# A two-layer graph kernel: the last tiles of the softmax sums in another order, and the weighting of the exponentials shared between VectorE and GpSimd

## The chip, the cores and the metric

One NeuronCore of a Trainium2 chip runs the program. The metric is the device time of one execution in microseconds (us); lower is better. All times here are medians of repeated executions, or come from one profiled execution.

## The reference, cut to what matters

The input is 512 nodes of 1024 features and 8192 edges (src, dst). Layer 0 is a graph layer with attention over edges, layer 1 a normalised aggregation. What the change touches is the softmax over the edges that end in one node and what it feeds:

```python
feat  = concat([h[src], h[dst]], axis=1)               # 8192 x 2048
e_f   = relu(feat @ W_kind + b_kind)                   # kinds hh, oo, ho by edge range
logit = (e_f @ W_a + b_a)[:, 0]
m     = segment_max(logit, dst)
ex    = exp(logit - m[dst])
den   = segment_sum(ex, dst)
z_f   = segment_sum((ex / den[dst])[:, None] * h[src], dst)
h_new = relu(concat([h, z_f])[:128] @ W_hn + b_hn)     # head rows
o_new = relu(concat([h, z_f])[128:] @ W_on + b_on)     # the other rows
```

The kernel doesn't keep alpha per edge. Edges of one kind between the same pair of nodes have the same logit, so it builds for each kind a dense 512x512 matrix of logits and one of edge counts. The attention matrix is then, row by row, the sum over three kinds of count * exp(logit - row max), divided by its row sum.

## The kernel before, in words

**Stages.** The products h @ W_ho, W_oo and W_hh run as "chunks" of eight weight slices each (`chunk`, L807; matmuls at L818); tables of the products go to HBM. GpSimd gathers the two table rows of each edge (`gather_src` L396, `gather_dst` L403, `gather_add` L410). The 64 edge tiles of 128 edges are numbered 0 to 51 (kind ho), 52 to 61 (kind oo), 62 and 63 (kind hh); tiles 0 to 61 are gathered. For a gathered tile, VectorE's `edge(q)` (L1154) makes the logits: an odd tile takes an addition of two gathered rows (L1161) and a multiply with a row sum (L1166), an even one the multiply alone, since its addition was made in the gather. `split_logits(a, b)` (L1180) adds the bias and cuts the logits into three bf16-exact parts, five small instructions. `logit_onehots(q)` (L1193) writes two one-hot matrices per tile (source and destination), by two TENSOR_SCALAR instructions at L1197, into one of four slots. ScalarE's `logit_parts(q)` (L611) then writes three copies of the destination one-hot, each scaled by one part of the logit (three ACTIVATE at L616). TensorE's `add_logits` (L862) waits for `s_part` and multiplies the parts with the source one-hot into PSUM banks 0 to 3 (L768), after which the slot is free (`s_ohu`).

**Order around the change.** Stages 14 and 15 come behind the last chunk (13) that needs weights beside the sums. All engines follow hand-written tables, keyed by (stage, k): `SUM_AT` (L485) says which tiles TensorE sums, `ONEHOT_AT` builds the one-hots one step ahead of it, `EDGE_AT` (L501), `SPLIT_AT` (L509) and `KIND_AT` (L512) place VectorE's `edge`, `split_logits` and `copy_kind`. In one step VectorE does `copy_kind`, then `edge`, then `split_logits`, then `logit_onehots`. `SUM_AT` has tiles 44 to 51 at (14,0) to (14,3), the two hh tiles at (14,5), 52 to 55 at (14,6) and (14,7), 56 to 59 at (15,0) and (15,1), 60 at (15,2) and 61 at (15,3). After the last tile of a kind TensorE closes the banks (L791) and VectorE reads them (`copy_kind`, four instructions at L1219); only then TensorE opens the banks for the next kind (L787).

**TensorE's queue** runs `head_rows(0)` (L957, matmuls at L966, the first half of a product for the 128 head rows) between chunk 13 and stage 14, and `head_rows(1)` behind stage 15. **ScalarE's queue** has `keep_second_halves((1,))` (L595, L601), which waits for the end of chunk 13, ahead of all `logit_parts` of stages 14 and 15.

**Weighting.** After the last `copy_kind`, the row maximum is made (L1336 to L1338), ScalarE makes twelve exponentials, four row blocks k by three kinds t (L705), and VectorE, per row block: three TENSOR_TENSOR_REDUCE at L1344 (multiply with the counts, row sum into `den3`), the addition of kind 1 to kind 0 (L1348), the sum of the three row sums (L1349), a reciprocal (L1350), and the addition of kind 2 (L1351), which releases ScalarE's scaling by the reciprocal (L709). TensorE transposes the result (L983) and uses it in the products at L996. In GpSimd's queue there are, behind the last gather, eight loads of h into SBUF (L455, L456), two bias loads behind the last tile's sum (L372), and then loads that wait for later stages.

Of the kernel before, what the change touches and what calls it, by code (L numbers as in the profile page):

```python
# [7 lines left out]
ALU = mybir.AluOpType  # L8
ACT = mybir.ActivationFunctionType
AX = mybir.AxisListType  # L10
# [11 lines left out]
TINY = 1e-30  # L22
# [3 lines left out]
def gnn_kernel(nc, x, src, dst, W_hh, b_hh, W_oo, b_oo, W_ho, b_ho, W_a, b_a,  # L26
# [3 lines left out]
    NM = N // P  # L30
    KT = D // P
    NN = D // FB
    ET = E // P
# [5 lines left out]
    with ExitStack() as ctx:  # L39
        def sem(name):  # L40
            return ctx.enter_context(nc.semaphore(name))
# [29 lines left out]
        logit_d = sb("logit_d", [P, 3, NM, N], F32)  # L71
        count_d = sb("count_d", [P, 3, NM, N], U16)
# [3 lines left out]
        onehot = sb("onehot", [P, OS, 4, N], BF16, over="topsum")  # L76
# [3 lines left out]
        iota_f = sb("iota_f", [P, N], FP16)  # L80
# [17 lines left out]
        node_f = sb("node_f", [P, ET, 3], F32)  # L98
# [6 lines left out]
        lgs = sb("lgs", [P, 3, ET], F32)  # L105
# [7 lines left out]
        den3 = sb("den3", [P, NM, 3], F32)  # L113
        den = sb("den", [P, NM], F32)
        rden = sb("rden", [P, NM], F32)
# [58 lines left out]
        s_part = sem("onehot_parts_ready")  # L174
# [33 lines left out]
        s_kfree = sem("kind_banks_free")  # L208
        s_mx = sem("row_max_ready")
        s_exp = sem("exp_done")  # L210
        s_rden = sem("row_sums_ready")
        s_att = sem("attention_ready")
        s_top = sem("top_banks_free")
# [135 lines left out]
        def _(pool):  # L349
# [21 lines left out]
            def bias(place, b):  # L371
                pool.dma_start(bias2[:, place, :], b.rearrange("(a d) -> a d", a=1).partition_broadcast(P)).then_inc(s_bias, 16)  # L372
# [84 lines left out]
            pool.wait_ge(s_ohu, OS + 2 * ET)  # L457
            bias(0, b_hn)
            bias(1, b_on)
            pool.wait_ge(s_deg, 2)  # L460
            pool.wait_ge(s_adjs, 2)
            pool.wait_ge(s_hnc, NN)
# [35 lines left out]
        for (c, k), qs in SUM_AT.items():  # L498
# [3 lines left out]
        EDGE_AT |= {divmod(8 * KT + 2 * i, KT): (24 + i,) for i in range(16)}  # L502
        EDGE_AT |= {(11, 7): (40,)}
        EDGE_AT |= {divmod(12 * KT + (3 * i) // 2, KT): (41 + i,) for i in range(10)}
        EDGE_AT |= {(14, k): (51 + k,) for k in range(KT)}
        EDGE_AT |= {(15, k): (59 + k,) for k in range(3)}
        assert [q for at_ in sorted(EDGE_AT) for q in EDGE_AT[at_]] == list(range(TG))
        ADJ_AT = {(6, 1): (0, 0), (6, 3): (0, 1), (6, 5): (1, 0), (6, 7): (1, 1), (7, 2): (2, 0), (7, 5): (2, 1)}
        SPLIT_AT = {(5, 7): (0, 7), (6, 7): (7, 14), (7, 7): (14, 19), (8, 7): (19, 24), (9, 7): (24, 29), (10, 7): (29, 34),  # L509
                    (11, 7): (34, 41), (12, 3): (TG, ET), (12, 7): (41, 46), (13, 7): (46, 51), (14, 0): (51, 52), (14, 3): (52, 54),  # L510
                    (14, 5): (54, 56), (14, 6): (56, 58), (15, 0): (58, 60), (15, 1): (60, 61), (15, 2): (61, 62)}
        KIND_AT = {(14, 5): 0, (14, 6): 2}  # L512

        SLOT = {q: i % OS for q, i in ORDER.items()}

        FIRST_EARLY = 2 * 2 * KT
        EARLY_BUILT = (0, 1, 2, 9, 3, 4, 5, 6, 7, 8)
# [10 lines left out]
        def _(act):  # L528
# [66 lines left out]
            def keep_second_halves(ms):  # L595

                for m in ms:
                    if m == 1:
                        chunk_done(act, CH_EDGE + 1)
                        act.wait_ge(s_st[3], 16 * CH_HH)  # L600
                        nc.scalar.copy(stage[:, 3, :], ps[:, NM + m, :]).then_inc(s_copied, 1)  # L601
                    else:
                        nc.scalar.copy(topsum[:, m, FB:D], ps[:, NM + m, :]).then_inc(s_copied, 1)
# [7 lines left out]
            def logit_parts(q):  # L611

                act.wait_ge(s_oh, ET - 2 * len(EARLY_AT) + ORDER[q] + 1)
                s = SLOT[q]
                for i in (1, 2, 0):
                    ins = nc.scalar.mul(onehot[:, s, 1 + i, :], onehot[:, s, 1, :], lgs[:, i, q:q + 1])  # L616
                ins.then_inc(s_part, 1)
# [74 lines left out]
            for q in range(CH_EDGE + 2):  # L692
                edge_chunk(q)
            q = CH_EDGE + 2
            keep_second_halves((1,))
            for at_ in SUM_AT:
                if at_[0] >= q:
                    for t in SUM_AT[at_]:
                        logit_parts(t)
            act.wait_ge(s_ohu, OS + 2 * ET)  # L700
            keep_second_halves((2, 3))
            act.wait_ge(s_mx, 1)
# [46 lines left out]
        def _(pe):  # L749
# [111 lines left out]

            def add_logits(q, place, s):  # L862

                pe.wait_ge(s_part, ORDER[q] + 1)
                accumulate(reg[0], place, onehot[:, s], 3)

            def sums(c, k):

                for q in SUM_AT.get((c, k), ()):
                    if q in (TG, T_HO):  # L870
                        pe.wait_ge(s_kfree, NM if q == TG else 2 * NM)
                        open_masked(2 if q == TG else 1)
                    if q % TC == 0 or q in (TG, T_HO):
                        reg[0] = codes(q // TC, TC)
                    add_logits(q, q % TC, SLOT[q])
                    if q in LAST_OF_KIND:
                        close_banks(s_kind)
# [79 lines left out]
            def head_rows(n):  # L957

                if n == 0:
                    pe.wait_ge(s_ht, 1)  # L960
                    pe.wait_ge(s_degin, 1)
                else:
                    pe.wait_ge(s_copied, base + 4)
                for k in range(KT):
                    pe.wait_ge(s_raw[k], (CH_EDGE + 2 + n) * 16 + 16)
                    nc.tensor.matmul(ps[:, NM + n, :], hT[:, k, :], raw[:, k, :], start=(k == 0), stop=(k == KT - 1)).then_inc(s_hn, 1)  # L966
                pe.wait_ge(s_hn, n * KT + KT)
                pe.sem_inc(s_hnc, 1)

            head_rows(0)  # L970
            for c in (14, 15):
                for k in range(KT):
                    sums(c, k)
            head_rows(1)
            pe.wait_ge(s_dinv, 1)
# [77 lines left out]
        def _(dve):  # L1053
# [5 lines left out]
            def step(ins):  # L1059

                chain[0] += 1
                ins.then_inc(s_v, 1)
                dve.wait_ge(s_v, chain[0])
# [129 lines left out]
            def logit_onehots(q):  # L1193

                dve.wait_ge(s_ohu, ET + ORDER[q] + 1)
                for j, e in ((0, 0), (1, 2)):
                    ins = nc.vector.tensor_scalar(onehot[:, SLOT[q], j, :], iota_f[:, :], node_f[:, q, e:e + 1], None, ALU.is_equal)  # L1197
                ins.then_inc(s_oh, 1)

            def inverse_counts(t, h):  # L1200
# [137 lines left out]
            nc.vector.tensor_scalar(nmx[:, :], mx[:, :], -1.0, None, ALU.mult).then_inc(s_mx, 1)  # L1338
            q = CH_EDGE + 2

            for k in range(NM):
                for t in range(3):
                    dve.wait_ge(s_exp, 3 * k + t + 1)
                    ins = nc.vector.tensor_tensor_reduce(out=logit_d[:, t, k, :], in0=logit_d[:, t, k, :], in1=count_d[:, t, k, :],  # L1344
                                                         scale=1.0, scalar=TINY if t == 0 else 0.0, op0=ALU.mult, op1=ALU.add,
                                                         accum_out=den3[:, k, t:t + 1])
                step(ins)
                nc.vector.tensor_tensor(logit_d[:, 0, k, :], logit_d[:, 0, k, :], logit_d[:, 1, k, :], ALU.add)  # L1348
                step(nc.vector.tensor_reduce(den[:, k:k + 1], den3[:, k, :], AX.X, ALU.add))  # L1349
                nc.vector.reciprocal(rden[:, k:k + 1], den[:, k:k + 1])  # L1350
                nc.vector.tensor_tensor(logit_d[:, 0, k, :], logit_d[:, 0, k, :], logit_d[:, 2, k, :], ALU.add).then_inc(s_rden, 1)  # L1351
            dve.wait_ge(s_deg, 2)
            nc.vector.tensor_copy(wrow[:, :], ps[:, 6, 0:NM]).then_inc(s_dinv, 1)
            for k in range(NM):
# [142 lines left out]
```

## Time and profile before

| | us |
|---|---|
| median of 3 executions (604.33 to 607.87) | 604.45 |
| the profiled execution, own time | 605.15 |
| its span in the profile | 603.4 |

The span is what the profile shows from the first to the last instruction of the core; 1.75 us of the execution's own time lie outside it. The profile gives each instruction's engine, line and duration, and for idle time the instruction whose end released the engine. PE is TensorE, DVE is VectorE, ACT is ScalarE, POOL is GpSimd. PEclk is the granted clock of TensorE as a share of full speed: 1.00 is 2.4 GHz, 0.50 is 1.2 GHz.

### The profile page before, as it was taken

How to read it: one execution, taken by the hardware profiler on the slowest of the kernel's cores; microseconds unless marked ns; L12 is line 12 of the kernel's file. 1: busy time of each engine (PE TensorE's matmuls, PEld its weight loads, DVE VectorE, ACT ScalarE, POOL GpSimd, SP SyncE). 2: the span in 40 equal slices, each digit the busy share in tenths (PEclk: the TensorE clock that was granted, in tenths of full speed). 3: DMA queues.
4: the chain of work that ended last, by engine and by line, in shares of the span. 5: the costliest groups of instructions: out<-in, count | busy, mean ns of one | idle time of the engine just before them, and what ended most of it. 6: DMA issues, size and time to landing. Idle time of an engine off the chain costs nothing.

```text
span 603.4 us, 7247 instructions
## 1 busy us (share of the span) xinstructions
PE 533.4 (88%) x2132; PEld 365.2 (61%) x2137; DVE 425.3 (70%) x910; ACT 278.1 (46%) x439; POOL 184.4 (31%) x177
## 2 busy tenths in 40 slices
PE   1799989999997999979998699965686999999997
PEld 1688857777763677634443377621135887878885
DVE  6756337865479699598868877667957469888352
ACT  0723431211225998756427556474865355225200
POOL 3260030008366565354738464532120100000000
PEclk9799989999998899999998799987575999999999
DMA  8897275349999999999999999987092537403121
GB/s 307 316 386 285 113 263 208 132 151 264 390 335 349 364 290 313 355 317 352 368 342 319 365 317 317 305 242 174 7 375 107 210 115 265 144 2 99 41 87 52
DMA packets 55838, 146.95 MB, mean 244 GB/s; under 512 B 6770, under 2 KB 6898, under 8 KB 55410
## 3 DMA queue, kind: packets, MB, share of 16 engines
q0 software_dynamic: 22352, 81.28, 42.9%
q1 hardware_dynamic: 27936, 54.54, 25.5%
q10 hardware_dynamic: 5506, 10.56, 4.7%
q8 instruction: 27, 0.44, 0.3%
q14 instruction: 17, 0.14, 0.1%
HBM read 127.47 MB, written 18.87 MB: 243 GB/s over the span
## 4 chain that ended last, share of the span: by engine, by line
PE 69%; DVE 18%; ACT 7%; issue 4%; ACTq 1%; DMA 1%; DVEq 0%
PE ps L818 37%; PE ps L768 9%; PE ps L908 8%; PE ps L996 4%; PE ps L1049 4%; ACT onehot L616 4%; PE ps L1027 3%; DVE gath L1166 2%; DVE ring_l L1141 2%; DVE onehot L1197 1%; DVE logit_d L1344 1%; DVE gath L1161 1%; PE ps L791 1%; PE ps L966 1%; DVE logit_d L1219 1%
## 5 line engine op out<-in xcount | busy, mean ns | idle before, releaser
L818 PE MATMUL ps<-ring_h,actT_h 128*128 128x512 f32 x376 | 161.4, 429 | 4.5 <-DVE actT_l L1136 3.1
L616 ACT ACTIVATE onehot<-onehot,lgs 128x512 bf16<-128x512 bf16 x192 | 122.4, 710 | 63.5 <-DVE onehot L1197 63.0
L818 PE MATMUL ps<-ring_l,actT_h 128*128 128x512 f32 x376 | 149.3, 397 | 0.0
L818 PE MATMUL ps<-ring_h,actT_l 128*128 128x512 f32 x376 | 149.3, 397 | 0.0
L560 ACT CAST ring_h<-raw 128x512 fp32r<-128x512 f32 x128 | 76.0, 621 | 92.6 <-PE ps L818 64.1
L1141 DVE TENSOR_TENSOR ring_l<-raw,ring_h 128x512 fp32r<-128x512 f32 x128 | 85.3, 687 | 38.8 <-ACT ring_h L560 29.3
L768 PE MATMUL ps<-onehot 128*128 128x512 bf16 x267 | 81.3, 419 | 33.9 <-ACT onehot L616 28.0
L400 POOL DMA_INDIRECT gath<-tab_a,tabl_i x62 | 68.8, 1110 | 133.0 <-DVE gath L1166 76.0
L1166 DVE SCALAR_TENSOR_TENSOR gath<-gath,wa_b 128x1024 f32<-128x1024 f32 x62 | 75.9, 1225 | 19.4 <-DMA gath<-tab_b,tabl_i 18.3
L818 PEld LDWEIGHTS ps<-ring_h,actT_h 128*128 128x128 f32 x376 | 72.6, 193 | 26.8 <-DVE actT_l L1136 3.3
L818 PEld LDWEIGHTS ps<-ring_h,actT_l 128*128 128x128 f32 x376 | 72.3, 192 | 16.1
L818 PEld LDWEIGHTS ps<-ring_l,actT_h 128*128 128x128 f32 x376 | 72.6, 193 | 14.7
L414 POOL DMA_INDIRECT gath<-tab_b,tabl_i x31 | 54.8, 1768 | 71.6 <-DMA tab_b<-stage 44.9
L768 PEld LDWEIGHTS ps<-onehot 128*128 128x128 bf16 x269 | 22.5, 102 | 86.4 <-issue 75.9
L1197 DVE TENSOR_SCALAR onehot<-iota_f,node_f 128x512 bf16<-128x512 f16 x128 | 39.4, 356 | 9.8 <-PE ps L768 9.1
L1161 DVE TENSOR_TENSOR gath<-gath 128x1024 f32<-128x1024 f32 x31 | 37.8, 1220 | 4.2 <-DMA gath<-tab_b,tabl_i 4.0
L407 POOL DMA_INDIRECT gath<-tab_b,tabl_i x31 | 33.4, 1078 | 9.4 <-issue 8.8
L908 PE MATMUL ps<-raw,featT_dst 128*128 128x512 f32 x64 | 30.0, 607 | 0.0
L908 PE MATMUL ps<-raw,featT_src 128*128 128x512 f32 x64 | 29.1, 592 | 0.0
L1089 DVE TENSOR_SCALAR onehot<-iota_f,node_f 128x512 bf16<-128x512 f16 x44 | 16.1, 365 | 15.9 <-PE ps L768 13.9
L1131 DVE TENSOR_TENSOR actT_l<-ps,actT_h 128x512 fp32r<-128x512 f32 x16 | 11.0, 690 | 14.3 <-ACT actT_h L550 14.3
L578 ACT COPY stage<-ps 128x512 f32<-128x512 f32 x16 | 9.4, 585 | 24.4 <-PE ps L818 19.0
(199 smaller groups left out, 632.9 us busy)
## 6 DMA issues: line engine op xcount, KB each, us to landing
raw<-in_L_gnn_W_ho_dram SPq DMA_DIRECT2D x32, 256.0 KB
raw<-in_L_gnn_W_oo_dram SPq DMA_DIRECT2D x32, 256.0 KB
raw<-in_L_gnn_W_hh_dram SPq DMA_DIRECT2D x32, 256.0 KB
raw<-in_L_gnn_W_on_dram SPq DMA_DIRECT2D x32, 256.0 KB
raw<-in_L_gnn_W_hn_dram SPq DMA_DIRECT2D x32, 256.0 KB
tab_a<-stage ACTq DMA_DIRECT2D x16, 256.0 KB
tab_b<-stage ACTq DMA_DIRECT2D x16, 256.0 KB
raw<-in_L_gnn_W_dram SPq DMA_DIRECT2D x16, 256.0 KB
```

The lines of the kernel that those rows point to most:

```text
L400: pool.indirect_dma_start(out=gath[:, c % GB, :], out_offset=None, in_=tab_a[0:kinds * N, :], in_offset=bass.IndirectOffsetOnAxis(ap=tabl_ ...
L407: pool.indirect_dma_start(out=gath[:, c % GB, :], out_offset=None, in_=tab_b[0:kinds * N, :], in_offset=bass.IndirectOffsetOnAxis(ap=tabl_ ...
L414: pool.indirect_dma_start(out=gath[:, c % GB, :], out_offset=None, in_=tab_b[0:kinds * N, :], in_offset=bass.IndirectOffsetOnAxis(ap=tabl_ ...
L560: nc.scalar.copy(ring_h[:, k, :], raw[:, k % RAW, :]).then_inc(s_high, 1)
L616: ins = nc.scalar.mul(onehot[:, s, 1 + i, :], onehot[:, s, 1, :], lgs[:, i, q:q + 1])
L768: mm = nc.tensor.matmul(ps[:, bass.ds((lo + j) & 3, 1), :].rearrange("p a n -> p (a n)"), rows[:, 1 + i, j * P:(j + 1) * P], rows[:, 0, :] ...
L818: mm = nc.tensor.matmul(ps[:, first + m, :], w, v, start=(k == 0 and i == 0), stop=(k == KT - 1 and i == 2))
L908: mm = nc.tensor.matmul(ps[:, b, :], featT[half][:, k, t * P:(t + 1) * P], raw[:, k, :], start=(half == 0 and k == 0), stop=(half == 1 and ...
L1141: nc.vector.tensor_tensor(ring_l[:, k, :], raw[:, k % RAW, :], f32(ring_h[:, k, :]), ALU.subtract).then_inc(s_low, 1)
L1161: nc.vector.tensor_tensor(gath[:, c % GB, :], gath[:, c % GB, :], gath[:, d % GB, :], ALU.add).then_inc(s_sum, 1)
L1166: nc.vector.scalar_tensor_tensor(out=gath[:, c % GB, :], in0=gath[:, c % GB, :], scalar=0.0, in1=wa_b[:, :], op0=ALU.max, op1=ALU.mult, ac ...
L1197: ins = nc.vector.tensor_scalar(onehot[:, SLOT[q], j, :], iota_f[:, :], node_f[:, q, e:e + 1], None, ALU.is_equal)
```

## The change

1. Edges: tile 52 joins tile 51 in step (14,0), and all later tiles are made one step earlier; tiles 60 and 61 are split together in (15,1).
2. For tiles 57, 59 and 61 (`SCALED`) VectorE itself writes the three scaled one-hots from `iota_f`, by three TENSOR_SCALAR with compare and multiply, in place of the one plain destination one-hot; ScalarE leaves these tiles out. TensorE waits for `s_oh` for them, and for the renumbered `s_part` (`PART_NO`) for the others.
3. `keep_second_halves((1,))` moves on ScalarE from ahead of stage 14 to behind the parts of step (14,3).
4. `head_rows(0)` moves on TensorE from ahead of stage 14 to ahead of the sums of step (14,2).
5. Weighting: VectorE's three instructions per row block become plain TENSOR_TENSOR multiplies. GpSimd adds kind 1 to kind 0. `row_sum(k)` on VectorE adds kind 2 with the row sum taken in the same instruction, adds TINY, and takes the reciprocal, which now releases ScalarE. It stands behind the first multiply of the next row block.

```diff
@@ gpsimd, behind the two bias loads
+            for k in range(NM):
+                pool.wait_ge(s_weight, 3 * k + 2)
+                nc.gpsimd.tensor_tensor(logit_d[:, 0, k, :], logit_d[:, 0, k, :], logit_d[:, 1, k, :], ALU.add).then_inc(s_pair, 1)
@@ tables
-        EDGE_AT |= {(14, k): (51 + k,) for k in range(KT)}
-        EDGE_AT |= {(15, k): (59 + k,) for k in range(3)}
+        EDGE_AT |= {(14, 0): (51, 52)}
+        EDGE_AT |= {(14, k): (52 + k,) for k in range(1, KT)}
+        EDGE_AT |= {(15, 0): (60,), (15, 1): (61,)}
-                    (14, 5): (54, 56), (14, 6): (56, 58), (15, 0): (58, 60), (15, 1): (60, 61), (15, 2): (61, 62)}
+                    (14, 5): (54, 56), (14, 6): (56, 58), (15, 0): (58, 60), (15, 1): (60, 62)}
+        SCALED = (57, 59, 61)
+        PART_NO = {q: i + 1 for i, q in enumerate(q for q in SUMS if q not in SCALED)}
@@ scalar
-            keep_second_halves((1,))
             for at_ in SUM_AT:
                 if at_[0] >= q:
                     for t in SUM_AT[at_]:
-                        logit_parts(t)
+                        if t not in SCALED:
+                            logit_parts(t)
+                    if at_ == (14, 3):
+                        keep_second_halves((1,))
@@ tensor, add_logits
-                pe.wait_ge(s_part, ORDER[q] + 1)
+                if q in SCALED:
+                    pe.wait_ge(s_oh, ET - 2 * len(EARLY_AT) + ORDER[q] + 1)
+                else:
+                    pe.wait_ge(s_part, PART_NO[q])
@@ tensor
-            head_rows(0)
             for c in (14, 15):
                 for k in range(KT):
+                    if (c, k) == (14, 2):
+                        head_rows(0)
                     sums(c, k)
@@ vector, logit_onehots
+                if q in SCALED:
+                    for i in range(3):
+                        ins = nc.vector.tensor_scalar(onehot[:, s, 1 + i, :], iota_f[:, :], node_f[:, q, 2:3], lgs[:, i, q:q + 1],
+                                                      ALU.is_equal, ALU.mult)
+                else:
+                    ins = nc.vector.tensor_scalar(onehot[:, s, 1, :], iota_f[:, :], node_f[:, q, 2:3], None, ALU.is_equal)
@@ vector, weighting
+            def row_sum(k):
+
+                dve.wait_ge(s_pair, k + 1)
+                dve.wait_ge(s_weight, 3 * k + 3)
+                step(nc.vector.scalar_tensor_tensor(out=logit_d[:, 0, k, :], in0=logit_d[:, 0, k, :], scalar=1.0, in1=logit_d[:, 2, k, :],
+                                                    op0=ALU.mult, op1=ALU.add, accum_out=den[:, k:k + 1]))
+                step(nc.vector.tensor_scalar(den[:, k:k + 1], den[:, k:k + 1], TINY, None, ALU.add))
+                nc.vector.reciprocal(rden[:, k:k + 1], den[:, k:k + 1]).then_inc(s_rden, 1)
+
             for k in range(NM):
                 for t in range(3):
                     dve.wait_ge(s_exp, 3 * k + t + 1)
-                    ins = nc.vector.tensor_tensor_reduce(...)
-                step(ins)
-                nc.vector.tensor_tensor(logit_d[:, 0, k, :], logit_d[:, 0, k, :], logit_d[:, 1, k, :], ALU.add)
-                step(nc.vector.tensor_reduce(den[:, k:k + 1], den3[:, k, :], AX.X, ALU.add))
-                nc.vector.reciprocal(rden[:, k:k + 1], den[:, k:k + 1])
-                nc.vector.tensor_tensor(logit_d[:, 0, k, :], logit_d[:, 0, k, :], logit_d[:, 2, k, :], ALU.add).then_inc(s_rden, 1)
+                    nc.vector.tensor_tensor(logit_d[:, t, k, :], logit_d[:, t, k, :], count_d[:, t, k, :], ALU.mult).then_inc(s_weight, 1)
+                    if k and t == 0:
+                        row_sum(k - 1)
+            row_sum(NM - 1)
```

## Rows read from the trace of the kernel before

**Rows 1.** Windows: us, then busy us (instructions) per engine, PEclk, DMA share, GB/s

```profile
core 0: us, PE busy (x) PEld busy (x) DVE busy (x) ACT busy (x) POOL busy (x), PEclk, DMA share, GB/s
...
388.00:396.00 8.00, 7.11 (x19) 2.82 (x18) 0.00 (x0) 7.93 (x13) 2.29 (x2) 1.00 0.94 272
...
404.00:412.00 8.00, 4.03 (x10) 1.17 (x10) 6.62 (x16) 4.50 (x8) 6.59 (x5) 0.51 0.84 207
```

**Rows 2.** Waits, 387 to 463 us: us in total, times, longest

```profile
ACT onehot L616 <- DVE onehot L1197: 13.0, 5, 5.0
...
PE ps L768 <- ACT onehot L616: 10.0, 6, 4.2
```

**Rows 3.** Timeline of TensorE, 378 to 475 us: start, duration, engine, line, operation

```profile
387.84 7.03 PE L966 MATMUL ps<-raw,hT 128*128 128x512 f32 x16
395.75 3.04 PE L768 MATMUL ps<-onehot 128*128 128x512 bf16 x12 [0.89 <-PE ps L966]
...
412.90 2.22 PE L768 MATMUL ps<-onehot 128*128 128x512 bf16 x6
...
439.59 1.46 PE L768 MATMUL ps<-onehot 128*128 128x512 bf16 x3 [1.75 <-ACT onehot L616]
...
442.55 8.33 PE L966 MATMUL ps<-raw,hT 128*128 128x512 f32 x16
```

**Rows 4.** Timeline of ScalarE, 372 to 475 us

```profile
388.04 0.58 ACT L601 COPY stage<-ps 128x512 f32<-128x512 f32 x1 [8.03 <-PE ps L818]
388.52 7.45 ACT L616 ACTIVATE onehot<-onehot,lgs 128x512 bf16<-128x512 bf16 x12
...
422.71 12.97 ACT L616 ACTIVATE onehot<-onehot,lgs 128x512 bf16<-128x512 bf16 x21 [5.00 <-DVE onehot L1197]
```

**Rows 5.** Timeline of VectorE, 372 to 443 us

```profile
380.40 1.38 DVE L1197 TENSOR_SCALAR onehot<-iota_f,node_f 128x512 bf16<-128x512 f16 x4
...
408.63 0.69 DVE L1219 CUSTOM_DVE_ANT_0 logit_d<-ps,logit_d 128x512 f32<-128x512 f32 x1 [1.35 <-PE ps L791]
...
411.07 1.22 DVE L1166 SCALAR_TENSOR_TENSOR gath<-gath,wa_b 128x1024 f32<-128x1024 f32 x1
...
416.02 0.69 DVE L1219 CUSTOM_DVE_ANT_0 logit_d<-ps,logit_d 128x512 f32<-128x512 f32 x1 [1.60 <-PE ps L791]
...
418.47 1.22 DVE L1161 TENSOR_TENSOR gath<-gath 128x1024 f32<-128x1024 f32 x1
...
421.00 0.23 DVE L1187 TENSOR_SCALAR lgr<-lg,ba 128x2 f32<-128x2 f32 x1
...
422.06 1.14 DVE L1197 TENSOR_SCALAR onehot<-iota_f,node_f 128x512 bf16<-128x512 f16 x4
...
442.79 0.69 DVE L1219 CUSTOM_DVE_ANT_0 logit_d<-ps,logit_d 128x512 f32<-128x512 f32 x1 [5.88 <-PE ps L791]
```

**Rows 6.** Groups by line and shape on VectorE: busy us, mean ns, idle before

```profile
L1119 DVE TENSOR_SCALAR hrow<-rows,mv,rstd 128x1024 f32<-128x1024 f32 x4 | 3.0, 808 | 0.0
```

**Rows 7.** Timeline of VectorE, the weighting, 446 to 461 us

```profile
446.71 0.69 DVE L1344 CUSTOM_DVE_ANT_0 logit_d<-logit_d,count_d 128x512 f32<-128x512 f32 x1 [0.79 <-ACT logit_d L705]
...
448.67 0.69 DVE L1348 TENSOR_TENSOR logit_d<-logit_d 128x512 f32<-128x512 f32 x1
449.28 0.15 DVE L1349 TENSOR_REDUCE den<-den 128x1 f32<-128x3 f32 x1
449.46 0.16 DVE L1350 RECIPROCAL rden<-den 128x1 f32<-128x1 f32 x1
...
450.13 0.68 DVE L1344 CUSTOM_DVE_ANT_0 logit_d<-logit_d,count_d 128x512 f32<-128x512 f32 x1
...
459.78 0.67 DVE L1351 TENSOR_TENSOR logit_d<-logit_d 128x512 f32<-128x512 f32 x1
```

**Rows 8.** Timeline of GpSimd, single instructions at both ends of the run

```profile
2.54 0.29 POOL L358 CAST ident_b<-ident 128x128 bf16<-128x128 f32 x1
...
3.29 0.09 POOL L364 MEMSET ones<- 128x1 f32 x1
...
29.22 6.39 POOL L380 DMA_INDIRECT hh_rows<-h_rows,hh_i  x1 [0.30 <-issue]
...
379.88 1.56 POOL L414 DMA_INDIRECT gath<-tab_b,tabl_i  x1 [0.31 <-issue]
```

More of the change, by code:

```diff
@@ L210, in gnn_kernel @@
         s_exp = sem("exp_done")
+        s_weight = sem("kinds_weighted")
+        s_pair = sem("two_kinds_summed")
         s_rden = sem("row_sums_ready")
@@ L1195, in logit_onehots @@
                 dve.wait_ge(s_ohu, ET + ORDER[q] + 1)
-                for j, e in ((0, 0), (1, 2)):
-                    ins = nc.vector.tensor_scalar(onehot[:, SLOT[q], j, :], iota_f[:, :], node_f[:, q, e:e + 1], None, ALU.is_equal)
+                s = SLOT[q]
+                ins = nc.vector.tensor_scalar(onehot[:, s, 0, :], iota_f[:, :], node_f[:, q, 0:1], None, ALU.is_equal)
+                if q in SCALED:
[4 more added lines that the diff above has]
+                    ins = nc.vector.tensor_scalar(onehot[:, s, 1, :], iota_f[:, :], node_f[:, q, 2:3], None, ALU.is_equal)
                 ins.then_inc(s_oh, 1)
@@ L1343, in _ @@
                     dve.wait_ge(s_exp, 3 * k + t + 1)
-                    ins = nc.vector.tensor_tensor_reduce(out=logit_d[:, t, k, :], in0=logit_d[:, t, k, :], in1=count_d[:, t, k, :],
-                                                         scale=1.0, scalar=TINY if t == 0 else 0.0, op0=ALU.mult, op1=ALU.add,
-                                                         accum_out=den3[:, k, t:t + 1])
-                step(ins)
-                nc.vector.tensor_tensor(logit_d[:, 0, k, :], logit_d[:, 0, k, :], logit_d[:, 1, k, :], ALU.add)
-                step(nc.vector.tensor_reduce(den[:, k:k + 1], den3[:, k, :], AX.X, ALU.add))
-                nc.vector.reciprocal(rden[:, k:k + 1], den[:, k:k + 1])
-                nc.vector.tensor_tensor(logit_d[:, 0, k, :], logit_d[:, 0, k, :], logit_d[:, 2, k, :], ALU.add).then_inc(s_rden, 1)
+                    nc.vector.tensor_tensor(logit_d[:, t, k, :], logit_d[:, t, k, :], count_d[:, t, k, :], ALU.mult).then_inc(s_weight, 1)
+                    if k and t == 0:
+                        row_sum(k - 1)
+            row_sum(NM - 1)
             dve.wait_ge(s_deg, 2)
```

## The prediction

> **What bounds the kernel now.** I read the windows first, to see where TensorE is not full, then the waits of that stretch, then the timelines of its engines. From 404 us TensorE does 4.03 us of work in 8 and its granted clock falls to 0.51, the lower of its two levels (1.2 GHz) [rows 1]: it waits. The waits say for whom: TensorE 10.0 us for ScalarE's scaled one-hots, and ScalarE 13.0 us for VectorE's plain ones [rows 2]. So between 388 us and the last read of the banks at 442.79 us the time is set by a chain that passes VectorE, ScalarE and TensorE in turn, through four slots. Two places stand out. ScalarE sits idle for 8.03 us until 388.04, on a copy that waits for chunk 13, while the one-hots of tile 44 had been there since about 381 us; the parts of tiles 44 to 47 are made only beside head_rows(0), and those of 48 to 51 only after it [rows 3, 4, 5]. And from 422.71 us ScalarE makes 21 scaled copies in one run of 12.97 us, seven tiles at 1.85 us each [rows 4]: there it is the bound. Behind 442.79 us the chain is VectorE's weighting, 446.71 to 460.45 [rows 7]. It sets the end: TensorE only transposes what that releases. Head_rows(1), 442.55 to 450.9 [rows 3], lies beside the weighting and is covered.
>
> **Stages 14 and 15, first part (edits 3 and 4).** I lay the new order along the clock of the trace. Chunk 13 still ends at about 388.0. ScalarE no longer waits for it: 44 from 381.2, 45 to 385.0. Edge 52 now stands ahead of the one-hots of 46 and 47 and costs 1.15 us (the row of 1.22 less its overlap [rows 5]); they are ready at 387.1 and 387.6, the parts at 389.0 and 390.9. TensorE does 44 and 45 at once and reaches 47 at about 391.6, for it starts 0.69 us behind the end of its parts (ScalarE's last part ended at 438.90, the tile's sum began at 439.59 [rows 3]). A tile takes 0.76 us (twelve matmuls in 3.04 [rows 3]): 392.4. Head_rows(0) takes 7.03 us: 399.5. In its shadow VectorE makes the one-hots of 48 and 49 behind edge 53 (390.1) and those of 50 and 51 once 47's slot is free, and ScalarE their parts, 390.9 to 398.4, four times 1.87. So behind head_rows(0) nothing is waited for: a gap of 0.9, four tiles 3.04, closing the banks 0.9 (sums end at 412.90 + 2.22, the read starts at 416.02 [rows 3, 5]), and copy_kind(0) starts at **404.3 in place of 408.63: 4.3 us earlier**. The moved copy (0.58 us) sits at about 398.5 on ScalarE, idle until the hh tiles are due, and only head_rows(1) needs it. What head_rows(0) releases is the load of eight weight slices for head_rows(1), 4.6 us later, used 40 us later. GpSimd's gathers run ahead: the last ones go out as slots come free, edge by edge, so they move with the edges, some 15 us ahead of use. Nothing else waits in either queue.
>
> The hh tiles: from the end of copy_kind(0) to copy_kind(2) is 4.95 us (411.07 to 416.02), opening, two tiles, closing [rows 5]. New: 406.75 + 4.95 = 411.7. VectorE in between has edge 57, now an odd one, 2.53 (418.47 to 421.00), a split 1.06, four one-hots 1.06 [rows 5]: ready at 411.4, just hidden. A later copy_kind(2) of some tenths is possible; it starts at 411.7, still 4.3 us early, and ends at 414.15.
>
> **Second part (edits 1 and 2).** From here VectorE alone sets the pace. Two even edges at 1.15, two odd at 2.53, three splits at 1.07 instead of four, and the one-hots: 54 and 55 four instructions, 56 and 57 six, 58 and 59 six, 60 two, 61 four. One costs 0.263 us (four in 1.06). The scaled form has two per-partition operands. The nearest row is the normalisation, the same form on 1024 f32 in 0.81 us [rows 6]; a slow path would cost one such instruction 0.6 instead of 0.26, nine of them 3 us. I take 0.263, since that row shows two such operands at two elements per cycle. Sum: 414.15 + 1.15 + 1.05 + 1.05 (54, 55 at 417.4) + 2.53 + 1.58 (57 at 421.5) + 1.15 + 1.1 + 1.58 (59 at 425.4) + 2.53 + 1.07 + 0.53 (60 at 429.6) + 1.05 (61 at 430.6). ScalarE has five tiles in this time, not eight, and is never behind: 60 from 429.6 to 431.55. TensorE: 60 at 432.25, 61 right behind at about 433.9, then, as from 439.59 to 442.79, 3.2 us to copy_kind(1): **437.1 in place of 442.79, 5.7 us earlier**. Slots: tile 59 needs 55's, 61 needs 57's; both are free two microseconds before. Bounds: if the close and tiles 48 to 51 go as in the best rows, 6.7; if everything behind head_rows(0) runs at the slow clock, 2 (below).
>
> **Weighting (edit 5).** Before: 13.74 us (446.71 to 460.45), 3.42 a row block [rows 7]. New on VectorE: twelve multiplies at 0.61 (the spacing of the plain addition, 448.67 to 449.28), 7.3; four row_sum: addition with accumulator 0.61, a hold of 0.12, the small addition 0.18, the reciprocal 0.08 until the next, 1.0 each, 4.0. Together 11.35, 2.4 less. But the addition on GpSimd is new, and no row shows it. By its rows a cast of 128 elements takes 0.29 and a fill of one 0.09 [rows 8]: 1.6 ns an element, so 512 elements with one input 0.9, and with two between 0.9 and 1.7. I take 1.2, since two inputs need not double the work. VectorE has 1.22 us of its own between the multiply that GpSimd waits for and row_sum(k), and behind the last row block only 0.61. If the two engines overlap fully, with 0.25 us of signals: three waits of 0.25 and one of 0.85, total 12.95, **0.8 us less**. If they take turns, each addition stands in full: 11.35 + 4 x 1.2 + 0.1 = 16.25, **2.5 us more**. The nearest rows: four one-hots took 1.38 us while GpSimd wrote descriptors (380.40, 379.88) and 1.14 without it [rows 5, 8]: the engines do hinder each other, though these are other kinds of instructions. I take turns as the likelier. Behind GpSimd's new waits stand only loads that wait for later stages in any case (front: adj, residual, last bias), so nobody is held by them.
>
> The Trainium skill, page "SBUF — State Buffer", section "Who interferes with whom", speaks against this edit: a VectorE instruction with two SBUF inputs and a GpSimd instruction that reads SBUF exclude each other, and the second to start stands still until the first is done. By it every multiply excludes the addition, which is the +2.5; if it did not hold, the -0.8. Of the price, "GPSIMD Engine Reference", section "Elementwise — side-by-side cycle accounting", gives about 2.6 cycles an element at 1.2 GHz for two inputs; an estimate from that page is 1.17 us, and the sum would be the same. No row here shows either.
>
> **Sum.** Profiled execution 605.15 (span 603.4 and 1.75 outside it) - 5.7 + 2.5 = 601.95; the median 604.45 lies 0.7 lower, so **601.2 us**. Behind 463 us TensorE is full, and what is early there stays early; the h loads go out with edge 61, 9 us earlier.
>
> **Rivals.**
> - *Overlap.* GpSimd's addition runs beside the multiplies: 604.45 - 5.7 - 0.8 = 598.0. For it: beside descriptor writing a one-hot lost only 0.06 us (1.38 less 1.14, by four [rows 5]). Against: writing descriptors reads no operands.
> - *The clock.* TensorE falls to 1.2 GHz in the sparse time before head_rows(0). Then that takes 8.33 (the second, which starts at the lower clock), tiles at 1.1 (six matmuls in 2.22 [rows 3]) 4.4, the close 0.9 more: copy_kind(0) at 407.9, 0.7 early, in all 2.1; with turns 604.45 - 2.1 + 2.5 = 604.85. Against: head_rows(0) comes 4 us behind a full chunk, and before the change the clock was still 1.00 up to 396 [rows 1].
> - *Slower: GpSimd's additions are long.* Their price A enters as 4A: the loss outweighs 5.7 from A = 2.0. At 3 us: 11.35 + 12.1 = 23.45, 9.7 more, 608.45. For it: one GpSimd record of 6.39 us among neighbours of 1 [rows 8], so an instruction there can be several times its own work; and VectorE's multiplies back to back may keep it off. Against: the fills and casts.
>
> **How the numbers follow.** Turns 0.45 (own range 599.5 to 603), overlap 0.3, clock 0.15, long additions 0.1. A change of 1% is 6.0 us, about what a measurement of this kernel can tell from none: faster below 598.4. That takes over half of overlap and a tenth of turns, and some of a wider gain, 0.25; slower above 610.5 only the worst of the last rival, 0.04. Range 596.4, overlap with the best of stage 14, to 604.9, the clock rival; outside lie the long additions and little else.
>
> **What would show it.** Right: ScalarE's L616 from 381, head_rows(0) at 392, copy_kind(0) at 404, no ScalarE run of 21, the last copy_kind near 437; in the weighting VectorE multiplies or GpSimd additions of 1.5 us and more, and a stage of 16 us. Wrong: additions of 1.2 us beside multiplies at 0.69 (overlap); head_rows(0) at 8.3 (clock); scaled one-hots above 0.5; a total gain over 8 us, which no term here can give.

## The result and the profile after

The changed kernel takes 601.24 us (median of 4 executions, 597.73 to 601.99) against 605.34 for the kernel before in the same comparison: a ratio of 0.9896, 95% interval 0.9857 to 0.9935. The forecast was 601.2. Ratios, here and below, leave out executions that took over 1.5% longer than the fastest of their kernel; of the run with no tile scaled that leaves three of ten (the median of all ten is 603.46 us), of version A three of six, and those two ratios say little. The profiled execution took 601.99 us, its span is 600.2, 3.2 below the span before.

That the total agrees to a few hundredths is luck. The forecast took 3.2 us off a median of 604.45; the medians of this comparison lie 4.1 apart, from 605.34. And in the profiled executions four differences make up the 3.2, two of which the forecast didn't have. To see them, count every time from the first instruction that TensorE runs behind chunk 13. That is 387.84 before (head_rows(0), [rows 3]) and 389.44 after. TensorE's timeline after:

```profile
389.44 1.47 PE L780 MATMUL ps<-onehot 128*128 128x512 bf16 x6
391.25 0.82 PE L780 MATMUL ps<-onehot 128*128 128x512 bf16 x3 [0.34 <-issue]
393.20 0.82 PE L780 MATMUL ps<-onehot 128*128 128x512 bf16 x3 [1.14 <-ACT onehot L626]
393.86 7.03 PE L981 MATMUL ps<-raw,hT 128*128 128x512 f32 x16
...
434.56 2.74 PE L780 MATMUL ps<-onehot 128*128 128x512 bf16 x6 [3.91 <-ACT onehot L626]
...
461.41 0.79 PE L1012 MATMUL ps<-attT_h,hrow_h 128*128 128x512 f32 x1 [0.76 <-DVE attT_l L1147]
```

Tiles 44 to 47 now run ahead of head_rows(0) (L981), as intended. VectorE's reads of the banks, three starts that answer to those in [rows 5], then the weighting that answers to [rows 7]:

```profile
405.91 0.69 DVE L1241 CUSTOM_DVE_ANT_0 logit_d<-ps,logit_d 128x512 f32<-128x512 f32 x1 [1.62 <-PE ps L803]
...
413.69 0.69 DVE L1241 CUSTOM_DVE_ANT_0 logit_d<-ps,logit_d 128x512 f32<-128x512 f32 x1 [0.73 <-PE ps L803]
...
422.59 1.06 DVE L1216 TENSOR_SCALAR onehot<-iota_f,node_f,lgs 128x512 bf16<-128x512 f16 x3
...
439.05 0.69 DVE L1241 CUSTOM_DVE_ANT_0 logit_d<-ps,logit_d 128x512 f32<-128x512 f32 x1 [5.92 <-PE ps L803]
...
442.97 3.60 DVE L1375 TENSOR_TENSOR logit_d<-logit_d,count_d 128x512 f32<-128x512 f32 x4 [0.79 <-ACT logit_d L717]
446.49 0.68 DVE L1367 SCALAR_TENSOR_TENSOR logit_d<-logit_d 128x512 f32<-128x512 f32 x1
...
457.64 0.69 DVE L1367 SCALAR_TENSOR_TENSOR logit_d<-logit_d 128x512 f32<-128x512 f32 x1 [1.16 <-POOL logit_d L464]
...
458.56 0.16 DVE L1370 RECIPROCAL rden<-den 128x1 f32<-128x1 f32 x1
```

The fourth multiply alone, and GpSimd's first addition:

```profile
444.81 1.76 DVE L1375 TENSOR_TENSOR logit_d<-logit_d,count_d 128x512 f32<-128x512 f32 x1
```

```profile
444.36 1.66 POOL L464 TENSOR_TENSOR logit_d<-logit_d 128x512 f32<-128x512 f32 x1 [5.69 <-DVE logit_d L1375]
```

All starts, counted from the end of chunk 13 (a start in the timeline less the first start behind chunk 13, the same for the runs of the next section):

| kernel | copy_kind(0) | copy_kind(2) | copy_kind(1) | first multiply | attention products |
|---|---|---|---|---|---|
| before | 20.79 | 28.18 | 54.95 | 58.87 | 75.30 |
| changed | 16.47 | 24.25 | 49.61 | 53.53 | 71.97 |
| difference | -4.32 | -3.93 | -5.34 | -5.34 | -3.33 |

So stages 14 and 15 gave 5.34 us and the weighting took 2.01 back: from the first multiply to the end of the instruction that releases ScalarE for the last time, 15.75 us here (442.97 to 458.72, the last reciprocal) against 13.74 (the last addition). Of the 3.33 us the span should have kept all. It kept 3.2, after two more differences: chunk 13 ended 1.60 us later in this execution, in code that is the same, and from the attention products to the end it took 138.8 us in place of 140.3, 1.5 less. The windows show where the latter comes from. First of the kernel before:

```profile
462.00:468.00 6.00, 5.24 (x14) 3.85 (x13) 3.86 (x5) 5.11 (x8) 0.00 (x0) 0.50 0.00 0
468.00:474.00 6.00, 6.00 (x26) 4.92 (x25) 3.50 (x5) 2.21 (x4) 2.09 (x4) 0.91 0.51 188
```

and of the changed one:

```profile
452.00:460.00 8.00, 2.69 (x10) 1.90 (x11) 5.49 (x14) 1.63 (x3) 3.30 (x2) 0.50 0.01 3
460.00:466.00 6.00, 5.24 (x18) 3.95 (x17) 3.58 (x5) 5.49 (x9) 0.00 (x0) 0.64 0.00 0
466.00:472.00 6.00, 6.00 (x28) 4.95 (x27) 3.76 (x6) 2.75 (x6) 2.14 (x4) 1.00 0.46 140
```

The column before the last two is the granted clock. Both kernels enter the products at the lower level, 1.2 GHz, behind a stretch in which TensorE mostly waits (2.69 us of work in the 8 us from 452 after the change, 3.33 in the 8 us from 455 before). After the change the level rises 2.7 us into the products (the spacing of matmuls falls from 0.43 to 0.23 us at 464.1), before it 5.7 us in (468.9). Three microseconds more at half the clock are 1.5 us, an estimate that accounts for the shorter rest. Since identical stages meet either level from one execution to the next (next section), this isn't shown to be an effect of the change.

### The profile page after: what moved, and what is told of

It is laid out like the page before. It is cut to its first block and busy times, and to the rows that moved or that the text cites. A ratio compares the mean times of both kernels' runs of the same rounds, so it can differ in the third digit from the quotient of the medians.

```text
span 600.2 us, 7235 instructions
## 1 busy us (share of the span) xinstructions
PE 531.2 (89%) x2132; PEld 364.9 (61%) x2137; DVE 428.1 (71%) x899; ACT 272.5 (45%) x430; POOL 194.2 (32%) x181
## 5 line engine op out<-in xcount | busy, mean ns | idle before, releaser
L626 ACT ACTIVATE onehot<-onehot,lgs 128x512 bf16<-128x512 bf16 x183 | 117.0, 710 | 71.2 <-DVE onehot L1219 70.7
L780 PE MATMUL ps<-onehot 128*128 128x512 bf16 x267 | 78.5, 411 | 31.3 <-ACT onehot L626 26.8
L923 PE MATMUL ps<-raw,featT_src 128*128 128x512 f32 x64 | 30.8, 622 | 0.0
L1105 DVE TENSOR_SCALAR onehot<-iota_f,node_f 128x512 bf16<-128x512 f16 x44 | 16.4, 372 | 16.3 <-PE ps L780 16.2
L1213 DVE TENSOR_SCALAR onehot<-iota_f,node_f 128x512 bf16<-128x512 f16 x64 | 24.3, 380 | 3.2 <-PE ps L780 2.6
L1219 DVE TENSOR_SCALAR onehot<-iota_f,node_f 128x512 bf16<-128x512 f16 x61 | 21.2, 347 | 0.0
L923 PEld LDWEIGHTS ps<-raw,featT_src 128*128 128x128 f32 x64 | 12.8, 199 | 13.1 <-issue 11.4
```

The source lines that it names most:

```text
L780: mm = nc.tensor.matmul(ps[:, bass.ds((lo + j) & 3, 1), :].rearrange("p a n -> p (a n)"), rows[:, 1 + i, j * P:(j + 1) * P], rows[:, 0, :] ...
L923: mm = nc.tensor.matmul(ps[:, b, :], featT[half][:, k, t * P:(t + 1) * P], raw[:, k, :], start=(half == 0 and k == 0), stop=(half == 1 and ...
L1213: ins = nc.vector.tensor_scalar(onehot[:, s, 0, :], iota_f[:, :], node_f[:, q, 0:1], None, ALU.is_equal)
```

## The experiments

Where a run and a time are compared, mind the spread. The executions of the kernel before lay between 600.2 and 610.7 us, and the end of chunk 13, which nothing here touches, between 383.0 and 393.8 us over the profiles. A term of 2 us is within that, so the counted starts decide and the times are given beside them. Ratios are against the kernel before. The counted starts have a spread too: with the stages 14 and 15 of the changed kernel, copy_kind(1) came at 48.29, 49.37, 49.51 and 49.61 in four profiles. What differs is TensorE's clock. Counted from copy_kind(2), VectorE's and ScalarE's starts on tile 60 repeat to 0.02 us in them, while six matmuls on the hh tiles took 1.77 us in one profile and 2.65 in another, and those on the last two tiles 2.28 or 2.74. So a difference of a microsecond in a read is only the order's if the matmuls ahead of it ran at the same level.

**The old weighting put back (edit 5 undone).**

```diff
-                    nc.vector.tensor_tensor(logit_d[:, t, k, :], logit_d[:, t, k, :], count_d[:, t, k, :], ALU.mult).then_inc(s_weight, 1)
+                    ins = nc.vector.tensor_tensor_reduce(...)
...
-                nc.gpsimd.tensor_tensor(logit_d[:, 0, k, :], logit_d[:, 0, k, :], logit_d[:, 1, k, :], ALU.add).then_inc(s_pair, 1)
```

> The changed kernel with the old weighting put back (edit 5 undone), edits 1 to 4 kept. In the changed kernel the weighting lasted 15.75 us (442.97 to 458.72) against 13.74 before, and one multiply per row block lasted 1.76 us. Turns (GpSimd's addition and VectorE's two-input multiplies exclude each other): the weighting falls back to 13.7 and the kernel is about 2.0 us faster than the changed one, near 599.2. Rival, overlap with the loss elsewhere (the accumulator in row_sum, the clock): the weighting is no shorter than 15 us and the time stays at 601. Stages 14 and 15 keep their 5.3 us in both.

Measured: the weighting is back at 13.78 us up to ScalarE's last scaling (15.79 in the changed kernel, 13.78 before, all to that same point). Attention products at 68.64, 3.33 us before the changed kernel's 71.97: 2.0 from the weighting and 1.3 from a shorter way to the last copy_kind (48.29 against 49.61), which the two runs below with the same stages don't repeat (49.37 and 49.51). Most of the 1.3 is TensorE's clock: copy_kind(0) to copy_kind(2) took 6.97 us for 7.78, and the last two tiles' six matmuls 2.28 for 2.74. In the times the run can't be told from the changed kernel: 600.68 us, ratio 0.9932 (0.9895 to 0.997). The expected 599.2 isn't met; it lies just below the interval, whose lower end is about 599.5 us.

**Edit 5 alone.**

```diff
+                nc.gpsimd.tensor_tensor(logit_d[:, 0, k, :], logit_d[:, 0, k, :], logit_d[:, 1, k, :], ALU.add).then_inc(s_pair, 1)
...
+                    nc.vector.tensor_tensor(logit_d[:, t, k, :], logit_d[:, t, k, :], count_d[:, t, k, :], ALU.mult).then_inc(s_weight, 1)
```

> The kernel before with edit 5 alone. Turns: the weighting lasts 15.7 to 16.2 us instead of 13.74, with multiplies of 1.76 us, and the kernel is 2.0 to 2.5 us slower than before, 0.3 to 0.4 per cent. Overlap: 12.9 us, 0.8 us faster.

Measured: 15.79 us up to ScalarE's last scaling, attention products at 77.51, 2.2 later than before; 609.15 us, ratio 1.0051 (1.0007 to 1.0095). In the counted starts this edit by itself is a loss. The time leans the same way, but the interval clears 1 by 0.0007 only, which I don't take as shown. VectorE's multiplies in it:

```profile
448.19 3.60 DVE L1358 TENSOR_TENSOR logit_d<-logit_d,count_d 128x512 f32<-128x512 f32 x4 [0.79 <-ACT logit_d L710]
```

Four multiplies in 3.60 us, where four at 0.61 and an overlap would be 2.5: one of them stood still for 1.1 us.

**GpSimd's work beside the old weighting, waited for by nobody.** Two runs, each with a single execution: an addition with its operands in SBUF, and a fill that reads nothing.

```diff
+            nc.gpsimd.memset(beside[:, :, :], 0.0).then_inc(s_pair, 1)
+            for k in range(NM):
+                pool.wait_ge(s_pair, k + 1)
+                pool.wait_ge(s_weight, 2 * k + 2)
+                nc.gpsimd.tensor_tensor(beside[:, 0, :], beside[:, 0, :], beside[:, 1, :], ALU.add).then_inc(s_pair, 1)
```

In the second the last line is `nc.gpsimd.memset(beside[:, :, :], 0.0).then_inc(s_pair, 1)`.

> Old weighting, edits 1 to 4 kept, and per row block one GpSimd addition of 128x512 f32 on a scratch tile of its own, released by the second multiply, for which VectorE doesn't wait until the stage is over. Nothing is computed from it. Turns: though nobody waits for the additions, the weighting lasts 13.7 plus four times 1.1 to 1.2, 18.1 to 18.5 us, with one instruction of about 1.8 us per row block. Rival (the loss of the changed kernel came from waiting for GpSimd's result, not from the shared reading): 13.7 us and no long instruction.

> As the run before, but GpSimd fills the scratch tile (128x1024 f32 written, nothing read) instead of adding. If only GpSimd's reading of operands shuts out VectorE's two-input instructions: the weighting stays at 13.7 us. If any GpSimd instruction does: longer by up to the fills' length, 3 us and more.

Measured, up to ScalarE's last scaling: 17.54 us with the additions and 13.78 with the fills, which is what it is without any GpSimd work. The additions' records, then the fills':

```profile
437.80 1.59 POOL L467 TENSOR_TENSOR beside<-beside 128x512 f32<-128x512 f32 x1 [4.80 <-DVE den L1369]
442.15 1.59 POOL L467 TENSOR_TENSOR beside<-beside 128x512 f32<-128x512 f32 x1 [2.76 <-DVE den L1369]
446.83 1.26 POOL L467 TENSOR_TENSOR beside<-beside 128x512 f32<-128x512 f32 x1 [3.09 <-DVE den L1369]
450.86 1.58 POOL L467 TENSOR_TENSOR beside<-beside 128x512 f32<-128x512 f32 x1 [2.77 <-DVE den L1369]
```

```profile
443.75 0.95 POOL L467 MEMSET beside<- 128x1024 f32 x1 [4.77 <-DVE den L1369]
447.17 0.95 POOL L467 MEMSET beside<- 128x1024 f32 x1 [2.46 <-DVE den L1369]
```

VectorE's addition of the same row block (L1375), first beside GpSimd's addition, then beside the fill of 443.75:

```profile
438.29 1.64 DVE L1375 TENSOR_TENSOR logit_d<-logit_d 128x512 f32<-128x512 f32 x1
```

```profile
444.28 0.69 DVE L1375 TENSOR_TENSOR logit_d<-logit_d 128x512 f32<-128x512 f32 x1
```

This settles that the two take turns. VectorE waits for no result here, and still each addition costs it 0.94 us ((17.54 - 13.78) / 4; I had expected 1.1 to 1.2, with one instruction of 1.8 per row block, and it was 1.62 to 1.64). A fill of 0.95 us, which overlaps the same instruction, costs nothing. So GpSimd's addition, which reads SBUF, shuts out VectorE's instruction with two SBUF operands, and the fill, which only writes, doesn't. VectorE's side wasn't varied: no instruction of it with one SBUF operand stood beside the additions. The Trainium skill, page "SBUF — State Buffer", section "Who interferes with whom", says just this of a VectorE instruction with two SBUF inputs: a GpSimd instruction that reads contends with it, one that only writes doesn't; these runs agree.

**Edits 3 and 4 alone, and edits 1 and 2 alone.**

```diff
-            head_rows(0)
             for c in (14, 15):
                 for k in range(KT):
+                    if (c, k) == (14, 2):
+                        head_rows(0)
                     sums(c, k)
```

> The kernel before with edits 3 and 4 alone: head_rows(0) and the kept second half later, nothing else. My steps: copy_kind(0) starts 20.8 us behind the first work after chunk 13 in the kernel before and 16.5 here, 4.3 us earlier; the rest of the two stages keeps its length, so the last copy_kind is 4.3 us early and the kernel 4.3 us faster, near 0.7 per cent. Rival (the second part's ScalarE run of seven tiles has slack and the edges edit carries the gain): under 2 us.

> The kernel before with edits 1 and 2 alone (edges one step early, tiles 57, 59 and 61 scaled by VectorE). My steps: nothing in the first part, since head_rows(0) and the kept copy stand where they were; in the second part the last copy_kind 1.4 us earlier, the kernel 1 to 1.5 us faster, 0.2 per cent. Rival (the last tiles are still bound by ScalarE's part of tile 60, which now waits for VectorE's extra instructions): 0 to 0.5 us.

| kernel | copy_kind(0) | copy_kind(2) | copy_kind(1) | attention products | ratio (95%) |
|---|---|---|---|---|---|
| late order alone | 15.43 | 21.83 | 48.59 | 68.93 | 0.9858 (0.9757 to 0.9959) |
| edges and scaled alone | 19.35 | 28.81 | 53.16 | 73.51 | 0.9998 (0.9947 to 1.0049) |

Both expectations miss. The late order alone is worth 6.4 us at copy_kind(1) and at the attention products, not 4.3; at the products that is more than the whole change gives (3.3). Its first read comes at 15.43, since edge 52 doesn't stand ahead of the one-hots of 46 and 47, and from there to the second read it takes 6.40 us in place of 7.39 before and 7.78 in the changed kernel. TensorE's timelines say why it is less than in the changed kernel. Late order alone:

```profile
405.58 1.76 PE L769 MATMUL ps<-onehot 128*128 128x512 bf16 x6
407.18 1.03 PE L792 MATMUL ps<-zeros_r 128*128 128x512 bf16 x4
```

The changed kernel:

```profile
409.64 2.65 PE L780 MATMUL ps<-onehot 128*128 128x512 bf16 x6
412.08 1.57 PE L803 MATMUL ps<-zeros_r 128*128 128x512 bf16 x4
```

The same six and four matmuls take 2.65 and 1.57 in place of 1.76 and 1.03: in the changed kernel part of them ran at the lower clock. Whether the sooner first read is why the clock held isn't shown; in two other runs with the changed kernel's edges the two tiles took 1.77 and VectorE's longer step (edge 57) bounded the second read at 6.97 instead.

Edits 1 and 2 alone move the last read by 1.8 us, against 1.4 expected, and by other steps than thought. 1.4 is gained ahead of copy_kind(0), which I had said wouldn't move; 0.9 of that is the closing of the banks, 1.03 us in place of 1.91, a matter of the clock. From there to copy_kind(2) it takes 9.46 us in place of 7.39, so 2.1 is lost, and behind it 2.4 is gained. On top of the late order the two edits bring nothing that these profiles show: copy_kind(1) at 49.37, 49.51 and 49.61, and once at 48.29, against 48.59.

**Which tiles VectorE should scale.** Edges as in the changed kernel.

```diff
-        SCALED = (57, 59, 61)
+        SCALED = ()
```

> The changed kernel with SCALED empty: ScalarE scales all tiles again, the edges stay one step early. In the changed kernel ScalarE's parts of 54 began at 419.00 and its last ones (tile 60) ended at 433.87; eight tiles in one run at 1.87 would end at 434.0. By my prediction's step (ScalarE is the bound there, sharing it out brings 1.4 us) this is 1 us or more slower than the changed kernel. Rival, from the trace after: VectorE's nine extra instructions sit in the same chain, so the last copy_kind moves by less than 0.7 us either way, and the kernel stays at 601.

The second with `SCALED = (61,)` and the old weighting:

> Old weighting, edits 1, 3 and 4, and SCALED of tile 61 alone. Its one-hots are the last of all, so only their scaling by VectorE takes ScalarE off the end of the chain, and tile 60 isn't delayed by the extra instructions for 57 and 59. Expected: ScalarE's last part ends 1 us earlier than in the changed kernel (433.87 - 419.00 behind its start with 54, here 13.8), the last copy_kind 0.7 to 1.2 us earlier, the kernel 598 to 599 with the old weighting. Rival (slots or TensorE's tiles bound it): no difference to the run with the old weighting and three scaled tiles.

| scaled by VectorE | copy_kind(2) | copy_kind(1) | between them | ratio (95%) |
|---|---|---|---|---|
| none | 24.25 | 48.75 | 24.50 | 0.984 (0.9785 to 0.9895) |
| 61 (old weighting) | 23.44 | 47.37 | 23.93 | 0.9833 (0.9774 to 0.9893) |
| 57, 59, 61 | 24.25 | 49.61 | 25.36 | 0.9896 (0.9857 to 0.9935) |

In all three rows TensorE was at its lower level in the last sums (three matmuls at 1.46 us or six at 2.74), so the stretches can be compared: scaling three tiles costs 0.9 us against scaling none, and 1.4 against the last alone. The first expectation misses both ways, since with none scaled the read comes 0.9 us earlier, not 1 later, and by more than the rival's 0.7. In the second ScalarE's last part ends 13.45 us behind its start with 54 (13.8 expected), and copy_kind(1) comes 2.2 us earlier (0.7 to 1.2 expected), 0.8 of it already at copy_kind(2); the time of 598.41 us is in its range.

Two marks that hold no matmul show the sum. VectorE's one-hots of tile 60 start 17.45 us behind copy_kind(2) with three tiles scaled (17.43 to 17.45 in five profiles), and 16.04 with none or with 61 alone: scaling 57 and 59 costs 1.4 us of VectorE's time. From ScalarE's start on tile 60 to copy_kind(1) it takes 7.13 us with 61 scaled and 7.68 without: scaling 61 gives 0.55 back. ScalarE in the changed kernel shows the same, and answers to its run of 21 in [rows 4]:

```profile
419.00 5.62 ACT L626 ACTIVATE onehot<-onehot,lgs 128x512 bf16<-128x512 bf16 x9 [2.74 <-DVE onehot L1219]
426.42 1.95 ACT L626 ACTIVATE onehot<-onehot,lgs 128x512 bf16<-128x512 bf16 x3 [1.80 <-DVE onehot L1219]
431.92 1.95 ACT L626 ACTIVATE onehot<-onehot,lgs 128x512 bf16<-128x512 bf16 x3 [3.56 <-DVE onehot L1219]
```

From being the bound it waits 1.80 and 3.56 us for VectorE. Its last part ends at 433.87, when eight tiles in one run from 419.00 would have ended at 434.0. And a scaled one-hot costs VectorE 0.32 us (422.59 to 423.56 by three), not 0.26.

**Versions from this.** Late order, tile 61 alone scaled, old weighting, with the edges of the kernel before (A), or one step early only from (14,4) on (B):

```diff
+        EDGE_AT |= {(14, k): (51 + k,) for k in range(4)}
+        EDGE_AT |= {(14, 4): (55, 56)}
+        EDGE_AT |= {(14, k): (52 + k,) for k in range(5, KT)}
+        EDGE_AT |= {(15, 0): (60,), (15, 1): (61,)}
```

A has the `SUM_AT`, `EDGE_AT` and `SPLIT_AT` of the kernel before; the lines above are B's.

A: 

> Late order (edits 3 and 4), edges and splits as in the kernel before, old weighting, tile 61 alone scaled by VectorE. Copy_kind(0) at 15.4, copy_kind(2) at 21.8; ScalarE still has its run of seven tiles, but the last tile no longer waits for a part, so the last copy_kind comes 1.3 to 1.7 us earlier than with the late order alone (48.6), at 47. Attention products at 67.4. The kernel 8 us faster than before. Rival (the scaled copies are as long on VectorE's chain as on ScalarE's): 48.3 or more.

B: 

> Late order (edits 3 and 4), old weighting, tile 61 alone scaled by VectorE, and the edges one step early only from (14,4) on, where tiles 55 and 56 share a step. Behind chunk 13's end: copy_kind(0) at 15.4 us as with the late order alone (edge 52 no longer stands ahead of the one-hots of 46 and 47), copy_kind(2) at 21.9 to 22.5, the last at 46 to 46.5 (48.6 with the late order alone, 49.6 in the changed kernel), the attention products at 66 to 67 (before 75.3, changed 72.0). The kernel 9 us faster than before, 1.5 per cent. Rival (the gather of tile 56 lands too late for (14,4), 1.2 us of waiting in an earlier run): copy_kind(0) later than 16 and the last at 47.5 or more.

| | copy_kind(0) | copy_kind(2) | copy_kind(1) | attention products | us, ratio (95%) |
|---|---|---|---|---|---|
| A | 15.43 | 21.91 | 45.92 | 66.27 | 600.31, 0.9891 (0.9843 to 0.9939) |
| B | 15.43 | 22.67 | 44.53 | 64.89 | 597.21, 0.9846 (0.9809 to 0.9883) |

Both are ahead of their expectation at the last read (47 for A, 46 to 46.5 for B), but that is TensorE's clock and not the order. The last two tiles and the closing in B, then in the run with 61 scaled and the edges of the changed kernel:

```profile
433.81 1.50 PE L778 MATMUL ps<-onehot 128*128 128x512 bf16 x6 [0.79 <-ACT onehot L624]
435.14 1.03 PE L801 MATMUL ps<-zeros_r 128*128 128x512 bf16 x4
```

```profile
432.49 2.74 PE L777 MATMUL ps<-onehot 128*128 128x512 bf16 x6 [0.79 <-ACT onehot L623]
435.02 1.91 PE L800 MATMUL ps<-zeros_r 128*128 128x512 bf16 x4
```

Up to ScalarE's part of tile 60 the two orders take the same 16.8 us from copy_kind(2); behind it B takes 5.04 and the other 7.12. So 2.1 us of B's last read come from the full clock; at the lower level it would be at 46.6, an estimate, and A, by the same reckoning (1.5 us), at 47.4. Whether these orders hold the clock more often isn't shown by one profile each.

B reaches the attention products 10.4 us before the kernel before and 7.1 before the changed one, 2.0 of the latter from the weighting, 2.1 from the clock and 3.0, the rest, from the order and the scaling. VectorE's three reads of the banks in B:

```profile
407.11 0.69 DVE L1239 CUSTOM_DVE_ANT_0 logit_d<-ps,logit_d 128x512 f32<-128x512 f32 x1 [1.61 <-PE ps L801]
414.35 0.69 DVE L1239 CUSTOM_DVE_ANT_0 logit_d<-ps,logit_d 128x512 f32<-128x512 f32 x1 [0.18 <-PE ps L801]
436.21 0.69 DVE L1239 CUSTOM_DVE_ANT_0 logit_d<-ps,logit_d 128x512 f32<-128x512 f32 x1 [3.83 <-PE ps L801]
```

At the second it waits 0.18 us, so edge 57 just fits, and at the last 3.83 in place of the changed kernel's 5.92. Against the kernel before both are faster in time. That B beats the changed kernel is shown by the counted starts, even with the 2.1 us taken off; the ratios' intervals still overlap. A's time misses its expectation of 8 us (600.31 against 605.91), B's 8.7 us meets its 9.

## Why the prediction was right, and where not

**First part: right to 0.02 us, for the changed kernel.** Chunk 13's end to copy_kind(0): 4.3 forecast, 4.32 measured. TensorE's 47 at about 391.6 came 3.76 us behind chunk 13 (393.20), forecast 3.8; head_rows(0) took the 7.03 of the rows. What the step didn't ask is what each edit does there. Edge 52 was priced at 1.15 and taken as part of the order; it costs 1.04 on the path (16.47 against 15.43), so edit 1 spoils a fifth of the 5.36 us that the late order gives there.

**"Opening, two tiles, closing": 4.95 us forecast, 5.34 measured** (408.35 to 413.69), because TensorE was at 1.2 GHz for part of it. VectorE was ready 0.73 us earlier, so "edge 57 just hidden" held.

**Second part: 1.4 us forecast, 1.41 measured** (5.34 less 3.93). The path was right: VectorE sets the pace there and ScalarE is never behind. Two errors cancel in it. A scaled one-hot costs 0.32 us and not 0.26, by which VectorE is about 0.3 late at tile 60, and TensorE does 61 right behind 60, 4.49 us from the start of 60 to the read (434.56 to 439.05) where the sum had 4.85. What the step didn't ask is whether the scaling was still wanted once the edges came a step earlier: it priced both edits as one. The runs part them, on top of the late order: edit 1 alone gives 2.3 us (24.50 against 26.77), and the three scaled tiles take 0.9 back.

**Weighting: 2.5 us forecast, 2.01 measured.** The mechanism, turns, is shown by the two runs beside the old weighting, and its direction by the edit alone. The mis-sized term is A: (15.75 - 11.35 - 0.1) / 4 = 1.08 us for 1.2. The records of 1.65 us are longer than that because they include GpSimd's own wait for the multiply that is running: from the end of that multiply (444.19 + 0.69) to the end of the addition (444.36 + 1.66) it is 1.14 us. In the run beside the old weighting the additions read 1.26 to 1.59, by when they started, and counted from the end of VectorE's running instruction 1.12 to 1.14. The rival of long additions falls: the first takes no longer than the others (1.66 and 1.65), so nothing like the one record of 6.39 us comes with it. The overlap rival falls by the multiply of 1.76 us. The clock rival falls for head_rows(0), which kept 7.03, but the clock did come in, one step later.

**The gathers "15 us ahead of use"** was too generous. VectorE waited 0.35 us for tile 56's in the changed kernel, and 1.16 in the run with tile 61 alone scaled. Both lie ahead of a longer wait for TensorE and cost nothing.

**"What is early there stays early"** missed the tail: 1.5 us less behind the attention products, with a clock that rose sooner, against chunk 13's end 1.6 us later by chance. They cancel. Each alone would have left the time in the range of 596.4 to 604.9.

## What to carry to other kernels

Before work goes to GpSimd, look at what VectorE does at that moment: if it runs instructions with two SBUF operands, and GpSimd's would read SBUF, the work isn't shared but queued, and even a result that nobody waits for costs nearly its full length (0.94 of 1.13 us here). Offload from an engine only as long as it is the bound at that spot; once another edit has moved the bound, the same offload turns into a loss (scaling tiles 57 and 59 cost 1.4 us, scaling 61, the last, gave 0.55). And when several edits go in together, time a mark close behind each in the trace: the whole change gave 3.3 us here, one of its parts alone 6.4. Read TensorE's level beside every such mark: in versions A and B it was worth 1.5 and 2.1 us that would have passed for the gain of the better order.

## What the runs showed that was not expected

- Identical code up to chunk 13 ends it anywhere from 383.0 to 393.8 us. The cause lies upstream and wasn't looked for. The spread of 10.8 us is twice as large as any term here.
- The clock that TensorE is granted at the start of the attention products rose 2.7 us in after the change and 5.7 us before; why one came sooner is open.
- Stages of the same code meet TensorE's two levels at different points from one execution to the next, and the last read of the banks moves by up to 1.3 us with it (48.29 to 49.61). What sets the moment isn't shown.
- A compare and multiply with two per-partition operands, 128x512, f16 in and bf16 out, costs 0.32 us on VectorE (422.59 to 423.56 by three); with one operand 0.26.
